# Attention output taken from kept queries, with gate rows, flux layout and order lists placed anew

## The reference, cut to what matters

```python
mod = (_silu(c) @ wmod).reshape(4, 6, 1, -1)
sa, ca, ga, sb, cb, gb = ...                       # six rows of each batch
ga = (2 * (ga >= 0) - 1) * jnp.maximum(jnp.abs(ga), 0.25)   # gb alike
h = _layernorm(x) * (1 + ca) + sa
q, k = _l2norm(heads(h @ Wq)), _l2norm(heads(h @ Wk));  v = heads(h @ Wv)
beta, fast_decay, slow_decay = sigmoid(h @ Wb), ...
hmid = silu(k_beta @ Wtf1 + btf1)                  # 4 values per head
token_flux = clip(sigmoid(hmid @ Wtf2 + btf2), 0.01, 0.99)
fast_w, slow_w = exp(cs[-1] - cs)                  # cs: sums of logs over the tokens
M_fast = einsum('bhld,bhle->bhde', k_beta * fast_w, v * beta) / fast_w.sum()
M_slow = ...
alpha = 0.5 + 0.3 * token_flux
o = alpha * (q @ M_fast) + (1 - alpha) * (q @ M_slow)
x = x + ga * (o @ Wo)
h = _layernorm(x) * (1 + cb) + sb
x = x + gb * ffn(h)        # 128 -> 352 -> 128; inputs of both products are quantized in blocks of 16
```

## Time and profile before

| what | us |
|---|---|
| median of 3 runs | 212.14 |
| lowest, highest | 210.84, 212.71 |
| span of the profiled execution | 209.9 |
| TensorE busy | 184.1 |
| VectorE busy | 174.6 |
| GpSimd busy | 152.7 |
| ScalarE busy | 144.9 |

### The profile page before, as it was taken

The page is one execution under the profiler, slowest core; times in us unless marked ns, Lnnn a source line. Parts: engine busy times, 40 slices in busy tenths (PEclk is TensorE's granted clock), DMA queues, the critical chain, the costliest instruction groups (busy, mean ns, idle before and its releaser), DMA issues.

```text
span 209.9 us, 3498 instructions
## 1 busy us (share of the span) xinstructions
PE 184.1 (88%) x948; PEld 134.0 (64%) x948; DVE 174.6 (83%) x436; ACT 144.9 (69%) x326; POOL 152.7 (73%) x187
## 2 busy tenths in 40 slices
PE   2899845999999999879669999899999896997994
PEld 1544433476788748539537777767788484694884
DVE  3997999837898999999999999899998897776840
ACT  2578999898997999969753637654836546663642
POOL 5477363968688878979996975978867968865460
PEclk9999999699999999999999999999999999999999
DMA  5980000000000000000000100000001000011011
GB/s 168 252 218 0 2 0 0 5 0 0 0 2 3 0 0 2 0 0 5 25 0 0 30 0 19 8 27 3 25 0 45 8 25 25 0 30 52 0 52 51
DMA packets 11499, 5.66 MB, mean 27 GB/s; under 512 B 1684, under 2 KB 11352, under 8 KB 11480
## 3 DMA queue, kind: packets, MB, share of 16 engines
q1 hardware_dynamic: 11168, 5.31, 9.1%
q10 hardware_dynamic: 312, 0.13, 0.2%
...
## 4 chain that ended last, share of the span: by engine, by line
PE 54%; ACT 15%; issue 12%; POOL 9%; DVE 6%; DMA 2%; SPq 0%; POOLq 0%; ACTq 0%; DVEq 0%
PE pa L1089 11%; PE pa L1166 6%; PE pg L1113 5%; PE pv L1168 5%; PE pa L1190 5%; PE pv L1130 4%; POOL q_o L487 3%; POOL q_r L475 3%; PE pa L1177 3%; PE pa L1139 3%; DMA wmod_sb<-in_L_wmod_dram 2%; ACT xn L680 2%; PE pv L1149 2%; ACT L526 2%; PE pa L1185 2%
## 5 line engine op out<-in xcount | busy, mean ns | idle before, releaser
L475 POOL TENSOR_TENSOR q_r<-q_x,q_rs 128x960 f32<-128x960 f32 (+2 forms) x18 | 29.6, 1645 | 14.3 <-DVE q_rs L960 14.3
L1089 PE MATMUL pa<-wcat,hT 128*128 128x496 f32 x64 | 31.5, 620 | 5.6 <-ACT sq L606 3.4
L487 POOL TENSOR_TENSOR q_o<-q_r,q_sp 128x960 f32<-128x960 f32 (+2 forms) x18 | 29.6, 1644 | 7.2 <-DVE q_r L971 6.4
L1166 PE MATMUL pa<-guT,hqT 128*128 128x352 f32 x64 | 25.3, 477 | 4.8 <-ACT hqT L697 4.7
L1190 PE MATMUL pa<-wdg,fqT 128*128 128x128 f32 x192 | 26.9, 276 | 0.0
L706 ACT ACTIVATE sgl<-pa 128x352 f32<-128x352 f32 x32 | 14.5, 461 | 15.1 <-PE pa L1166 12.8
L1168 PE MATMUL pv<-guT,hqT 128*128 128x352 f32 x64 | 24.3, 462 | 0.3 <-DVE oc L913 0.3
L438 POOL TENSOR_TENSOR vs<-kvg,cw 128x256 f32<-128x256 f32 x32 | 20.2, 658 | 5.7 <-DVE cw L864 5.7
L1190 PEld LDWEIGHTS pa<-wdg,fqT 128*128 128x128 f32 x192 | 24.0, 192 | 0.4 <-ACT fqT L714 0.2
L1089 PEld LDWEIGHTS pa<-wcat,hT 128*128 128x128 f32 x64 | 12.0, 204 | 16.6 <-ACT sq L606 6.8
L691 ACT ACTIVATE q_A<-q_r 128x960 f32<-128x960 bf16 (+2 forms) x18 | 16.0, 888 | 8.5 <-POOL q_r L475 5.3
(11 more groups left out here) (149 smaller groups left out, 446.5 us busy)
## 6 DMA issues: line engine op xcount, KB each, us to landing
...
```

Of the source, the lines that this page charges most:

```text
L475: g.tensor_tensor(blocks(q_r[:, s % 2, c]), blocks(q_x[:, s % 2, c]), spread(q_rs[:, s % 2, n]), ALU.mult)\
L487: g.tensor_tensor(blocks(q_o[:, s % 2, c]), blocks(q_r[:, s % 2, c]), spread(q_sp[:, s % 2, n]), ALU.mult)\
L1089: te.matmul(bank_a(("PP%d" % k, i))[:, 0:NCAT], hT[:, b, 2 * j + k, :], wcat[:, :], start=True, stop=True).then_inc(S["a_full"], 1)
L1166: te.matmul(bank_a(("G%d" % k, i))[:, 0:I], lhs, guT[:, 0, :], start=True, stop=True)\
```

## The change

It does five things.

- **Queries kept.** ScalarE now copies all 496 columns of PP (`qkvg` in place of `kvg`). O1 leaves TensorE: DVE multiplies the kept q by `coef`, twice 256 elements for a pair, both inputs in SBUF. O2 transposes the four blocks without summing; ScalarE copies 512 columns. O3 is four products instead of two, with `wm`, which is now the masked state times `wog` (two products of 128 columns for a batch). The V products have their operands swapped and are two of 128 columns instead of one of 256. The transpose of Wq goes. `hT` becomes a ring of three pairs.
- **Gate rows.** One product (MR) gives all rows of the four batches on four partitions; five DVE instructions on these apply the rule; MB spreads them to all partitions with a column of the identity as weights. `scB` and W0 go.
- **Flux layout.** `hin`, `hmid` have the four values per head outermost, so that each is read and written as one run of 128 elements, not with a step of four.
- **Banks.** The 16 fills of `pv` by O1 go.
- **Lists.** All four orders are new. In ScalarE's, steps that need the log/exp tables and steps that need the silu tables now alternate 12 times rather than 10: GE:1 stands behind GA:2, and GD:2 behind GS:2, ahead of the first gate F1:0.

```diff
     "scalar": """
+        dma:0 WK:0 CT:0 CM:0 PX:0 PX:1 KW:0 PX:2 PP:0 PP:1 PX:3 PP:2 PX:4 PP:3 PX:5 PP:4 PX:6 GA:0 PX:7 PP:5
+        W1:0 GD:0 PP:6 PX:8 GS:0 MB:0 GE:0 PX:9 PP:7 PP:8 PP:9 O2:0 PX:10 PX:11 GA:1 PP:10 PP:11 PX:12 GD:1
+        PX:13 O2:1 GG:0 GS:1 O2:2 GA:2 L1:0 O2:3 PP:12 PP:13 GE:1 W3:0 QA:4 L1:1 O2:4 GS:2 GG:1 PX:14 L1:2
+        GD:2 PX:15 PP:14 QA:5 N4:0 PP:15 F1:0 L1:3 O2:5 GA:3 QA:6 N4:1 O2:6 F1:1 L1:4 N4:2 F1:2 L1:5 QA:7 F3:0
+        GE:2 O2:7 QA:8 F4:0 GG:2 GD:3 N4:3 GS:3 F1:3 O2:8 L1:6 N4:4 F1:4 F3:1 QA:9 F4:1 L1:7 QA:10 GE:3 O2:9
+        N4:5 F3:2 F1:5 L1:8 F4:2 F3:3 N4:6 O2:10 QA:11 F1:6 F3:4 F4:3 N4:7 QA:12 L1:9 O2:11 F1:7 F3:5 N4:8
+        L1:10 O2:12 F1:8 QA:13 GG:3 O2:13 F4:4 QA:14 F3:6 F4:5 N4:9 L1:11 F1:9 F3:7 F4:6 N4:10 QA:15 L1:12
+        O2:14 F1:10 O2:15 L1:13 N4:11 F1:11 QA:16 F3:8 F4:7 F3:9 QA:17 L1:14 F4:8 N4:12 F3:10 F1:12 N4:13
+        L1:15 F1:13 QA:18 F4:9 F4:10 F3:11 QA:19 F4:11 N4:14 F1:14 N4:15 F3:12 F1:15 QA:20 F3:13 QA:21 F4:12
...
     "vector": """
+        P0:0 MV:0 XN:0 XN:1 XN:2 P0:1 XN:3 PP:0 P0:2 PP:1 PP:2 W1:0 GA:0 PP:3 GB:0 P0:3 MR:0 PP:4 PP:5 GK:0
+        GF:0 GE:0 PP:6 GY:0 O1:0 O1:1 GA:1 PP:7 W2:0 PP:8 GB:1 PP:9 GG:0 GK:1 O1:2 PP:10 PP:11 GA:2 O1:3 O3:0
+        GE:1 GB:2 GF:1 L1:0 O3:1 GK:2 O3:2 L1:1 PP:12 Q:4 PP:13 GG:1 GY:1 O1:4 L1:2 O1:5 QT:4 O3:3 Q:5 O1:6
+        O3:4 GE:2 PP:14 GF:2 L1:3 QT:5 PP:15 F1:0 GA:3 Q:6 GB:3 O3:5 O1:7 GK:3 QT:6 L1:4 F1:1 L1:5 Q:7 O3:6
+        F1:2 Q:8 QT:7 GY:2 GG:2 QT:8 O3:7 GF:3 L1:6 O1:8 O1:9 GE:3 F1:3 L1:7 Q:9 F1:4 Q:10 QT:9 O3:8 QT:10
+        O1:10 L1:8 F1:5 Q:11 O3:9 GY:3 QT:11 F1:6 Q:12 O3:10 L1:9 O1:11 QT:12 GG:3 F1:7 L1:10 O1:12 O1:13 Q:13
+        F1:8 Q:14 QT:13 O3:11 O3:12 L1:11 QT:14 F1:9 Q:15 L1:12 O3:13 O1:14 O1:15 QT:15 L1:13 F1:10 O3:14 Q:16
+        F1:11 Q:17 QT:16 L1:14 QT:17 O3:15 F1:12 L1:15 Q:18 F1:13 Q:19 QT:18 QT:19 F1:14 Q:20 F1:15 Q:21 QT:20
+        QT:21""",
     "gpsimd": """
+        P0:0 P0:1 XN:4 XN:5 XN:6 P0:2 KC:0 XN:7 XN:8 GC:0 XN:9 GB:0 V0:0 XN:10 V1:0 V2:0 P0:3 XN:11 V3:0 GF:0
+        XN:12 GO:0 XN:13 W2:0 GC:1 GO:1 GB:1 V0:1 O3:0 V1:1 V2:1 V3:1 O3:1 L1:0 GB:2 GF:1 QR:4 O3:2 XN:14
+        XN:15 GC:2 L1:1 QO:4 GO:2 O3:3 QR:5 O3:4 W3:0 V0:2 V1:2 L1:2 V2:2 QO:5 L1:3 QR:6 O3:5 GB:3 V3:2 QO:6
+        GF:2 L1:4 QR:7 GH:0 GC:3 QR:8 O3:6 L1:5 QO:7 QO:8 O3:7 L1:6 V0:3 QR:9 GO:3 V1:3 QR:10 QO:9 L1:7 O3:8
+        GH:1 QO:10 V2:3 QR:11 O3:9 V3:3 L1:8 QO:11 QR:12 O3:10 GF:3 L1:9 QO:12 L1:10 QR:13 QR:14 QO:13 O3:11
+        O3:12 L1:11 QO:14 QR:15 O3:13 L1:12 QO:15 L1:13 QR:16 O3:14 GH:2 QR:17 QO:16 L1:14 QO:17 O3:15 L1:15
+        QR:18 QR:19 QO:18 QO:19 QR:20 GH:3 QR:21 QO:20 QO:21""",
...
-                if b >= KRING and j == 0:
-
-                    act.wait_ge(S["g_full"], slot_g[("M", b - KRING)] + 1)
-                    act.wait_ge(S["hin0"], b - KRING + 1)
-                    act.wait_ge(S["zb"], b - KRING + 1)
+                if b >= KRING:
+                    act.wait_ge(S["qc"], 2 * (i - KRING * NP_) + 2)
+                    if j == 0:
+                        act.wait_ge(S["g_full"], slot_g[("M", b - KRING)] + 1)
+                        act.wait_ge(S["hin0"], b - KRING + 1)
+                        act.wait_ge(S["zb"], b - KRING + 1)
                 for k in range(2):
                     t = bank(("PP%d" % k, i))
                     n = 2 * i + k
-                    a.activation(kvg[:, n % (KRING * T), :], t[:, D:NCAT], ACT.Copy).then_inc(S["kvg"], 1)
+                    a.activation(qkvg[:, n % (KRING * T), :], t[:, 0:NCAT], ACT.Copy).then_inc(S["kvg"], 1)
                     if i >= 2 and k == 0:
                         act.wait_ge(S["ss"], (i - 2) + 1 + (i - 2) // NP_)
...
-                    a.activation(hmid[:, :, :, j], hin[:, :, :, j], ACT.Silu, bias=btf1_b[:, j:j + 1]).then_inc(S["hmid"], 1)
+                    a.activation(hmid[:, j], hin[:, j], ACT.Silu, bias=btf1_b[:, j:j + 1]).then_inc(S["hmid"], 1)
...
-                    act.wait_ge(S["v_full"], slot_v[("PO", NP_ * (b - 1) - 1)] + 1)
+                    act.wait_ge(S["v_full"], slot_v[("Y", NP_ * (b - 1) - 1)] + 1)
...
-                t = bank(("OT", i))
+                t = bank(("QCT", i))
                 if i >= 2:
                     act.wait_ge(S["v_full"], slot_v[("Y", i - 2)] + 1)
-                a.activation(oT[:, i % 2, :], t[:, 0:2 * D], ACT.Copy).then_inc(S["a_free"], 1)
+                a.activation(qcT[:, i % 2, :], t[:, :], ACT.Copy).then_inc(S["a_free"], 1)
...
-            def W0(_):
-
-                dve.wait_ge(S["a_free"], slot_a[("MB%d" % (NB - 1), 0)] + 1)
-                v.tensor_scalar(mb[:, :, 2, :], mb[:, :, 2, :], 1.0, None, ALU.add).then_inc(S["mbe"], 1)
-                for k, col in enumerate((0, 3)):
-                    gcol = mb[:, :, col, :]
-                    v.tensor_scalar(mb_sgn[:, :, k, :], gcol, 0.0, 2.0, ALU.is_ge, ALU.mult).then_inc(S["mbe"], 1)
-                    dve.wait_ge(S["mbe"], 2 + 4 * k)
-                    v.scalar_tensor_tensor(gcol, mb_sgn[:, :, k, :], 1.0, gcol, ALU.subtract, ALU.mult)\
-                        .then_inc(S["mbe"], 1)
-                    dve.wait_ge(S["mbe"], 3 + 4 * k)
-                    v.tensor_scalar(gcol, gcol, 0.25, None, ALU.max).then_inc(S["mbe"], 1)
-                    dve.wait_ge(S["mbe"], 4 + 4 * k)
-                    v.scalar_tensor_tensor(gcol, mb_sgn[:, :, k, :], 1.0, gcol, ALU.subtract, ALU.mult)\
-                        .then_inc(S["mbe"], 1)
+            def MR(_):
+
+                t = bank(("MR", 0))[0:NB, :].rearrange("b (m d) -> b m d", m=4)
+                v.tensor_scalar(mrow_s[:, :, :], t[:, 0:4:3, :], 0.0, 0.5, ALU.is_ge, ALU.subtract).then_inc(S["mrow"], 1)
+                dve.wait_ge(S["mrow0"], 1)
+                v.tensor_copy(mrow[0:NB, 1, :], t[:, 1, :]).then_inc(S["mrow"], 1)
+                v.tensor_scalar(mrow[0:NB, 2, :], t[:, 2, :], 1.0, None, ALU.add).then_inc(S["mrow"], 1)
+                dve.wait_ge(S["mrow"], 3)
+                v.scalar_tensor_tensor(mrow_a[:, :, :], mrow_s[:, :, :], 4.0, t[:, 0:4:3, :], ALU.mult, ALU.mult)\
+                    .then_inc(S["v_free"], 1)
+                dve.wait_ge(S["v_free"], slot_v[("MR", 0)] + 1)
+                v.scalar_tensor_tensor(mrow[0:NB, 0:4:3, :], mrow_a[:, :, :], 0.5, mrow_s[:, :, :], ALU.max, ALU.mult)\
+                    .then_inc(S["mrow"], 1)
...
-                t = bank(("PO", i))
                 dve.wait_ge(S["coef"], 2 * b + 2)
                 if i >= 2:
-                    dve.wait_ge(S["a_full"], slot_a[("OT", i - 2)] + 1)
-                v.tensor_tensor(oc[:, i % 2].rearrange("p t a (h d) -> p (t a h) d", d=DK),
-                                t[:, :].rearrange("p (n d) -> p n d", d=DK),
-                                coef[:, b % 2, 2 * j:2 * j + 2].rearrange("p t a h -> p (t a h)").unsqueeze(2)
-                                .to_broadcast([P, 4 * H, DK]), ALU.mult).then_inc(S["v_free"], 1)
+                    dve.wait_ge(S["a_full"], slot_a[("QCT", i - 2)] + 1)
+                for k in range(2):
+                    v.tensor_tensor(qc[:, i % 2, k].rearrange("p a (h d) -> p a h d", d=DK),
+                                    qkvg[:, (2 * i + k) % (KRING * T), 0:D].rearrange("p (h d) -> p h d", d=DK).unsqueeze(1)
+                                    .to_broadcast([P, 2, H, DK]),
+                                    coef[:, b % 2, 2 * j + k].unsqueeze(3).to_broadcast([P, 2, H, DK]),
+                                    ALU.mult).then_inc(S["qc"], 1)
...
+            def MR(_):
+                a_done(("CT", 0))
+                pe.wait_ge(S["wmod"], 16)
+                te.matmul(bank_v(("MR", 0))[0:NB, :], scT[:, :], wmod_sb[:, 2 * D:6 * D], start=True, stop=True)\
+                    .then_inc(S["v_full"], 1)
+
             def MB(_):
-                pe.wait_ge(S["scB"], 1)
-                pe.wait_ge(S["wmod"], 16)
+                v_done(("MR", 0))
+                pe.wait_ge(S["mrow"], 4)
                 for b in range(NB):
-                    te.matmul(bank_a(("MB%d" % b, 0))[:, :], scB[:, b, :], wmod_sb[:, 2 * D:6 * D],
-                              start=True, stop=True).then_inc(S["a_full"], 1)
+                    te.matmul(bank_a(("MB%d" % b, 0))[:, :], ident[:, b:b + 1].to_broadcast([P, P]),
+                              mrow[:, :, :].rearrange("b m d -> b (m d)"), start=True, stop=True).then_inc(S["a_full"], 1)
...
-                    last = te.matmul(t[:, 0:2 * D], kvg[:, (b % KRING) * T + n, 0:D],
-                                     vs[:, n].rearrange("p a d -> p (a d)"), start=(n == 0), stop=(n == T - 1))
+                    for m in range(2):
+                        last = te.matmul(t[:, m * D:(m + 1) * D], vs[:, n, m, :], qkvg[:, (b % KRING) * T + n, D:2 * D],
+                                         start=(n == 0 and m == 0), stop=(n == T - 1 and m == 1))
                 if q == NP_ - 1:
                     last.then_inc(S["g_full"], 1)
 
             def GG(b):
```

(42 more changed lines are left out.)

120 lines of the change are left out of this document (46 added, 74 removed).

## The result

The changed kernel takes 215.75 us at the median of four runs (214.23 to 217.02), the kernel before 212.25 beside it: a ratio of 1.018 (95% interval 1.010 to 1.026). It is slower, where 209.5 was forecast. Its profiled execution has a span of 212.5 us.

What follows compares the result with a forecast made beforehand. It took ScalarE and TensorE as tied limits up to the first gate, VectorE and TensorE behind it. Terms 0 - 1.1 - 1.5 = -2.6 gave a span of 207.3, with the profile's 2.2 offset 209.5 us; range 205.6 to 216.

Steps and rivals of the forecast that it cites:

- the first rival: Behind the first gate, GpSimd blocks VectorE's new O1 products, the second of two waiting; +3.1 us net, 215.2; chance 0.25.
- Every sign: TensorE busy near 179, ScalarE 152, twelve table loads, V0:0 near 31, first gate 77 to 80, O1 products 0.42 to 0.65.
- the step "0 us": Ahead of the first gate: ScalarE's +5.4 us is absorbed by idle time and an earlier start; gate stays at 78.5.
- 3.2 less there: VectorE ahead of the first gate: W0 and scB go, MR's five instructions come; net -3.2 us.
- The blocked products: VectorE behind the first gate: new O1 products wait for GpSimd, 0.35 us a pair, +3.2 us for nine pairs.
- the step "-1.1 - 1.5 = -2.6": Behind the first gate: -1.1 us from TensorE and VectorE averaged, -1.5 from half of TensorE's waits before O1 and O2.
- The mean of two full engines: Behind the first gate: TensorE's -4.3 and VectorE's +2.1 us, each at 90% or over, averaged to -1.1.
- TensorE's term: TensorE over the whole kernel: products saved and added sum to -5.3 us of 184, -4.3 of it behind the first gate.
- The -0.5 that I took for batch 3: VectorE's flux sum hz of batch 3: the middle between -0.9 us if the step of four is the cause and 0 if GpSimd.
- The table loads, 2.6 us in my sum: ScalarE before the first gate: two more table loads of 1.28 us each, +2.6 us.
- The second rival: ScalarE ahead of the first gate: half of its +5.4 us isn't absorbed, +2.7, and the -2.6 is gone: 212.2; chance 0.20.

Runs made afterwards that it cites:

- the narrow copies: The changed kernel with ScalarE's copies at their old widths (q not copied, one tile of two of the transposed queries): 215.13 us, ratio 1.014.
- the zeroing's move: The changed kernel with GpSimd's zeroing of a corner of wdT (W3:0) behind QR:7 instead of ahead of batch 2's V products: 213.12 us, ratio 1.002.

## Why the prediction was wrong

The measured 215.75 lies inside my range and beside the first rival's 215.2. Both are luck: the range was drawn around other mechanisms, and the rival's 3.1 us came from coefficient products that weren't held. Every sign that I named for being right was there or close, too: TensorE at 180.8, ScalarE at 149.9, twelve loads, V0:0 at 32.4, the gate at 79.6, the products at 0.49. They watched the parts that I had priced, and the loss lay between them.

**Ahead of the gate** the step "0 us" failed. The order of the parts was sound: V0:0 on GpSimd started at 32.4 (31 said) and O3:0 at 53.3 (51), and ScalarE ran at 97 to 98% from 20 to 80 us. The gate came 1.1 late in these traces and 1.9 at like clock, inside the range, and the narrow copies show 0.7 to 1.3 of it as ScalarE's width. VectorE, which I had at 3.2 less there, was busy 60.0 us for 56.0: `hz` has 2.8 us more, `kb` 1.5, both held. I had priced that hold for the new products behind the gate and for nothing ahead of it. The rest lay behind it: 1.6 us more were lost to F1:1, in a place that my sum didn't look at since I had put the border of the stages on the gate.

**The blocked products** are the step whose mechanism held and whose place was wrong. I priced the hold at 0.17 us for each of the new products; they lose 32 x (0.494 - 0.415) = 2.5 us in all, 0.08 each (415 is their median), and in no place that counts. Rival 1 needed 0.6 a pair and got 0.16. But its sign was right, for I had asked only what GpSimd does to the new instructions, and not what the new GpSimd list does to those that were there. One `hz`, held for 2.9 us in front of the one product that frees a bank, made 2.6 of the 3.5 us. A mean price by instruction can't show that; the hold falls on one instruction, and its worth depends on what is queued behind it. The Trainium skill, SBUF — State Buffer, section Who interferes with whom, says that the engine that comes second is blocked for the whole of the other's instruction. The trace differs in the length: 3.27 us are five instructions of GpSimd, not one. Where it says that on this chip a `tensor_reduce` never contends, the trace agrees: in the changed kernel `ss`, reduced from SBUF, took 0.67 us beside a V product (at 79.75) and 0.67 beside nothing (at 51.91).

**Behind the gate** the step "-1.1 - 1.5 = -2.6" failed. From F1:0 to the end the two traces show +1.5 instead (132.9 us for 131.4): +1.6 up to F1:1, by the hold, and from there 0, 120.8 us for 120.9. The mean of two full engines was no estimate of anything. 5.9 us less of TensorE, or 5.0 less of VectorE or of ScalarE, shorten the stretch behind F1:1 by nothing that can be told; 8.9 less of GpSimd give 1.2, all in the last 30 us. A busy share of 90% showed how full the engines are, and not that they are the limit. What sets the pair loop wasn't found by relieving one engine at a time and stays open; a chain of hand-overs in the order of the lists is what is left, and no run shows it. TensorE's term itself was near: it was to lose 5.3 us and shows 3.3 less, with its low clock in the two traces at different places.

**`hz`** at 549 ns with the layout alone says GpSimd, and not the step. The -0.5 that I took for batch 3 came, but for another reason: in the new lists no GpSimd instruction runs beside these three, and they take 1.05 us instead of 1.62. The table loads, 2.6 us in my sum, gave nothing back when two were removed, in an order that cost something of its own. The second rival, *ScalarE swallows it*, described the stage behind the gate better than the forecast did, but it ended at 212.2, with no loss.

Of the loss 2.6 us are shown by the zeroing's move. What remains is 1.0 to 1.2 at like clock (211.8 and 213.8 against 210.6 and 212.8), of which ScalarE's width is shown for some 0.2 to 0.7; the rest is open. No version that computes all of the result beats the kernel before beyond its interval: the best are its own, with the flux layout (0.998) and with the zeroing ahead of V (1.000).
